# A two-layer transformer kernel on one core: the first batch's stack transfers, the weight pieces and the raw score pairs laid out anew over the steps of phase 1

## Reference

```python
# layer 0: gated MLP with quantised hidden values and ternary weight
scale = cond @ norm_w.T + 1.0
h = x * (scale[:, None, :] * rsqrt(mean(x * x) + EPS))
val, gate = split(h @ up_w.T, 2)
h = val * gelu(gate)
x = act_quant(h) @ weight_quant(down_w).T + x
# layer 1: attention over 16 heads of width 16, then a SwiGLU MLP
a = gamma * rmsnorm(x) + beta
q, k, v = a @ W_q.T, a @ W_k.T, a @ W_v.T
x = x + alpha * (softmax(scale * q @ k.T) @ v) @ W_o.T
f = gamma2 * rmsnorm(x) + beta2
x = x + alpha2 * ((silu(f @ gate_w.T) * (f @ hidden_w.T)) @ out_w.T + out_b)
```

## Time and profile before

| what | value |
|---|---|
| three timed runs | 1126.82, 1130.36, 1130.57 us; median 1130.36 us |
| profiled execution | 1129.7 us, its span from the first to the last instruction 1127.9 us |
| mean granted PE clock of the span | 0.961 |
| busy in the span | PE 1050.0 us (93%), DVE 770.8, ACT 578.9, POOL 293.8 |
| phase 1 | 0 to about 279.6 us |

### The profile page before, as it was taken

One profiled execution on the slowest core, in us unless ns is written; L12 is line 12 of the kernel. 1 busy time (PEld: TensorE's weight loads), 2 busy tenths in 40 slices (PEclk: granted clock), 3 DMA queues, 4 the chain that ended last, 5 costly groups with the idle time before them and its releaser, 6 DMA issues.

```text
span 1127.9 us, 18491 instructions
## 1 busy us (share of the span) xinstructions
PE 1050.0 (93%) x5864; PEld 659.5 (58%) x5864; DVE 770.8 (68%) x1224; ACT 578.9 (51%) x1168; POOL 293.8 (26%) x280
## 2 busy tenths in 40 slices
PE   6999999996899999989999998999999899899868
PEld 4777777764433545655664565566456556645656
DVE  5877776885565687668658767865876686676132
ACT  5577765553454456455445535654564464356221
POOL 2344442220000132232213223222322232032233
PEclk9999999997999999999999999999999999979889
DMA  9232217111430613224050323405032240500100
GB/s 286 86 94 75 76 57 131 62 52 39 76 48 11 109 18 41 72 55 56 10 117 15 42 69 58 56 10 117 17 40 71 56 56 10 99 1 2 52 0 19
DMA packets 58800, 66.65 MB, mean 59 GB/s; under 512 B 10992, under 2 KB 43832, under 8 KB 58752
## 3 DMA queue, kind: packets, MB, share of 16 engines
q1 hardware_dynamic: 44160, 48.80, 20.4%
q10 hardware_dynamic: 14592, 17.25, 7.9%
HBM read 27.73 MB, written 12.61 MB: 36 GB/s over the span
## 4 chain that ended last, share of the span: by engine, by line
PE 80%; DMA 9%; DVE 6%; issue 2%; ACT 2%; POOL 0%; ACTq 0%; SPq 0%; POOLq 0%; DVEq 0%
PE bank L1092 18%; PE bank L359 14%; PE bank L945 10%; PE bank L926 10%; PE bank L1136 9%; DMA k_stack<-hid 6%; PE raw_pair L885 6%; PE bank L810 4%; PE bank L861 2%; PE bank L382 2%; DVE rowmax L893 2%; PE bank L1208 2%; PE bank L403 1%; DMA k_stack<-split 1%; DMA up_st<-up_wT 1%
## 5 line engine op out<-in xcount | busy, mean ns | idle before, releaser
L934 ACT ACTIVATE probs<-bank 128x512 f32<-128x512 f32 x512 | 282.5, 598 | 250.6 <-PE bank L926 248.4
L893 DVE TENSOR_REDUCE rowmax<-raw_pair 128x2 f32<-128x1024 f32 x256 | 313.2, 1223 | 133.9 <-PE raw_pair L885 133.9
L885 PE MATMUL raw_pair<-k_stack,q_stack 48*128 48x512 f32 x512 | 178.2, 471 | 35.1 <-DMA k_stack<-hid 17.8
L359 PE MATMUL bank<-up_w,xs_part 128*128 128x512 f32 x768 | 199.9, 411 | 5.2 <-POOL xs_part L337 5.1
L926 PE MATMUL bank<-q_stack,k_stack 50*128 50x512 f32 x512 | 196.4, 455 | 1.4 <-issue 1.2
L359 PEld LDWEIGHTS bank<-up_w,xs_part 128*128 128x128 f32 x768 | 144.4, 194 | 38.3 <-POOL xs_part L337 5.9
L945 PE MATMUL bank<-probs,v_ext 128*17 128x512 f32 x1024 | 140.8, 622 | 0.3
L926 PEld LDWEIGHTS bank<-q_stack,k_stack 50*128 50x128 f32 x512 | 81.4, 190 | 81.5 <-issue 57.6
L1122 POOL TENSOR_TENSOR hid<-scratch,hid 128x512 fp32r<-128x512 f32 x64 | 82.4, 1288 | 159.3 <-ACT hid L1118 159.3
L1092 PE MATMUL bank<-xf_part,gate_w 128*128 128x512 f32 x384 | 109.1, 421 | 4.9 <-POOL xf_part L1082 4.1
L1092 PEld LDWEIGHTS bank<-xf_part,gate_w 128*128 128x128 f32 x384 | 69.2, 193 | 69.5 <-issue 52.8
(11 more groups left out here) (127 smaller groups left out, 1259.2 us busy)
## 6 DMA issues: line engine op xcount, KB each, us to landing
q_stack<-split SPq DMA_DIRECT2D x48, 128.0 KB, 4.7
q_stack<-hid SPq DMA_DIRECT2D x48, 128.0 KB, 5.3
xk<-xT SPq DMA_DIRECT2D x32, 128.0 KB, 2.0
xt<-x_tok SPq DMA_DIRECT2D x32, 128.0 KB, 2.5
x_spill<-x1t ACTq DMA_DIRECT2D x32, 128.0 KB, 1.7
xa_spill<-xa ACTq DMA_DIRECT2D x32, 128.0 KB, 2.2
x_in<-xa_spill SPq DMA_DIRECT2D x8, 512.0 KB, 5.2
k_stack<-split ACTq DMA_DIRECT2D x32, 128.0 KB, 7.9
```

The costliest lines, as they stand in the source:

```text
L359: last = nc.tensor.matmul(bank[j][:], xs_part[a][:, m % 2, k, :], up_w[w][:, k, col + j * W:col + (j + 1) * W], start=(i == 0), stop=(i == ...
L885: mm = nc.tensor.matmul(raw_pair[:, half, :], q_stack[rows, slot, qt * P:(qt + 1) * P], k_stack[rows, slot, :], start=True, stop=True)
L893: nc.vector.reduce_max(rowmax[:, e:e + RAWS + 1:RAWS], raw_pair[:], AX.X).then_inc(raw_read, 1)
L934: nc.scalar.activation(probs[:, (kt % 2) * J + j, :], score_bank[c % 3][:], ACT.Exp).then_inc(exp_done, 1)
```

## The change

The change touches phase 1 alone. The weight pieces keep one a step at steps 3 and 4 and go two a step from step 5 to step 11, and the last at step 12 (before: one a step, steps 3 to 19). The load, split, fill and projection of batch 0 are four steps earlier (the load one step). The stack transfers of SP are spread: two ahead of the loads in each of steps 19 to 22; ACT's four go two a step at steps 19 and 20. The raw pairs go one a step from step 23 to step 33 (before: steps 25 to 34, with two at step 32). In steps 0 and 1 the first slice of the up weight (`up_high_act(0)`, `up_low_dve(0)`) goes behind the first tile's scaling instead of ahead of it.

```diff
-        HIGH_AT = 3
-        LOW_AT = HIGH_AT + 1
-        XA_AT, SPLIT_AT, ONES_AT, QK_AT, STACK_AT = 12, 17, (21, 22), (20, 21), 23
-        RAW_STEPS = {25: 1, 26: 1, 27: 1, 28: 1, 29: 1, 30: 1, 31: 1, 32: 2, 33: 1, 34: 1}
+        def pieces_at(n):
+            return [i for i in range(len(PIECES)) if n == (3 + i if i < 2 else 5 + (i - 2) // 2)]
+        XA_AT, SPLIT_AT, ONES_AT, QK_AT, STACK_AT = 11, 13, (15, 16), (16, 17), 19
+        RAWS_AT = 23
         def raws_before(n):
-            first = sum(count for step, count in RAW_STEPS.items() if step < n)
-            return range(first, first + RAW_STEPS.get(n, 0))
+            return (n - RAWS_AT,) if 0 <= n - RAWS_AT < AHEAD else ()
+        STACK_SP = [(0, half, r) for half in range(2) for r in range(ROWS // HD)] + [(1, half, 0) for half in range(2)]
...
-            elif n == STACK_AT:
+            elif 0 <= n - STACK_AT < 4:
                 sp.wait_ge(stack_ones, 2)
-                stack_sp(sp, 0, (0, 0))
+                for w, half, r in STACK_SP[2 * (n - STACK_AT):2 * (n - STACK_AT) + 2]:
+                    sp.wait_ge(pair_free[w], credited(pair_free[w], 1))
+                    stack_dma(sp, 0, w, half, r)
...
             if n == 0:
                 load_small_act(act)
-                up_high_act(act, 0)
             elif n == 1:
-                for i in range(1, len(CHUNKS)):
+                for i in range(len(CHUNKS)):
                     up_high_act(act, i)
-            if 0 <= n - HIGH_AT < len(PIECES):
-                late_high_act(act, n - HIGH_AT)
+            for i in pieces_at(n):
+                late_high_act(act, i)
...
-            if 0 <= n - LOW_AT < len(PIECES):
-                late_low_pool(pool, n - LOW_AT)
+            for i in pieces_at(n - 1):
+                late_low_pool(pool, i)
```

More of the change, by code:

```diff
@@ L746, in before_dve @@
                 scale_dve(dve)
-                up_low_dve(dve, 0)
             elif n == 1:
-                for i in range(1, len(CHUNKS)):
+                for i in range(len(CHUNKS)):
                     up_low_dve(dve, i)
```

## The result

The changed kernel took 1118.42 us in the median (1114.58 to 1119.71, five runs), the kernel before, beside it on the same chip, 1129.96 us (1125.93 to 1130.57): a ratio of 0.9906, with a 95% interval from 0.9878 to 0.9934. It is faster by more than 0.5%. The forecast was 1121.0 us, range 1117 to 1126. A second measurement of the same kernel (last experiments) gave 1120.89 us against 1127.53 (0.9944 [0.9911, 0.9976]), that is between 0.2 and 0.9% less. Two slow executions of the kernel before (1132.37 and 1135.92 us) are left out of the second comparison.

A forecast was written before the change was run, and what follows sets the result against it. PE was taken to bound phase 1, with holes at steps 23 and 32. Gains of 2.49, 5.08 and 1.48 us sum to 9.05: profiled 1129.7 becomes 1120.65, 1121.3 as median; forecast 1121.0, range 1117.0 to 1126.0.

The forecast's parts named there:

- to the start of step 22 (pieces, head, first transfers): Start of phase 1: doubled weight pieces, reordered first weight slice and spread stack transfers, each priced at 0.
- step 22 to the pair of step 33: Ten steps of 7.78 us, then 7.35 us to the pair: 255.77 instead of 264.82, 9.05 us less.
- drain, from there to the first score: End of phase 1, 14.8 us with PE mostly waiting: change taken as 0, bounded by 1.5 us either way.
- Rival 1: Stack's stall stays in another step, contention with the loads being the cause: 3.6 us not regained, 1124.6; chance 0.09.
- rival 5: Change does less: a pair still waits as DVE runs late in step 30, 3 us, 1124.0; chance 0.03.
- second hole: Step 32: second raw pair waits 4.57 us for the first's maximum; 5.08 us plus 1.48 of slow clock to regain.
- first hole: Step 23: PE runs dry on a late tile load; 3.6 us of stall and slow clock regained, net 2.49.
- The load of tile 23 stands behind eight stack transfers: On SP: load goes out at 176.89, behind transfers beginning at 171.07; tile scaled 6.65 us after issue.
- are the same instructions in other steps: Preparations moved four steps earlier; POOL's heaviest becomes step 15, with a split and a fill, covered by idle time.
- Rival 3: Doubled weight pieces on POOL block DVE in each of seven steps: 8.3 us in all, 1129.3; chance 0.04.
- Rival 2: Gain given back to the clock in drain and phase 2: two more slow groups, 3.0 us, 1124.0; chance 0.10.
- rival 4: Spread transfers delay loads, PE stalls in each of steps 19 to 22, 3.6 us each: 1135.4; chance 0.03.

The follow-up runs named there:

- old_raws: Changed kernel with the raw pairs at the steps of before (25 to 34, two at step 32); 1128.69 us, ratio 1.0001.
- single_raws: Kernel before with one raw pair a step, steps 25 to 35, and nothing else; 1125.79 us, ratio 0.9968.
- block19: Changed kernel with SP's eight stack transfers as one block ahead of the loads of tile 19; 1119.85 us, ratio 0.9907.
- block21: Changed kernel with SP's eight stack transfers as one block ahead of the loads of tile 21; 1120.05 us, ratio 0.9911.
- late_fill_spread: Changed kernel with the fills of ones late (second at step 18), transfers still two a step; 1120.02 us, ratio 0.9923.
- late_fill_block: Changed kernel with the fills of ones late (second at step 18) and SP's eight transfers in one block at step 19; 1124.87 us, ratio 0.9979.
- late_fill_again: Same kernel as late_fill_block, no further edit, profiled a second time; profiled execution 1122.51 us.
- pieces_only: Kernel before with the weight pieces two a step and nothing else of the change; 1130.08 us, ratio 1.0037.

## Why the prediction was right

| term of the forecast | forecast | first profile after | second profile |
|---|---|---|---|
| to the start of step 22 (pieces, head, first transfers) | 0 | -1.45 us | +0.16 us |
| step 22 to the pair of step 33 | -9.05 us | -9.10 us | -9.07 us |
| drain, from there to the first score | 0, bound 1.5 | -0.42 us | -0.37 us |
| phase 2 | 0 | -4.13 us | -2.82 us |

**The sum of step 22 to step 33** held to 0.05 us in both profiles: one pair a step gives steps of 7.78 us, both holes are closed, the shift on DVE at step 30 costs nothing, and the slow clock goes with the holes. Rival 1 (the stall stays) and rival 5 (a pair still waits) did not come. For the second hole, two pairs in one step on one buffer, the reason was right too: `old_raws` brings it back (a wait of 4.56 us) and `single_raws` takes it out.

**The reason for the first hole was half the reason.** The step "The load of tile 23 stands behind eight stack transfers" named the order on SP, and rival 1 set contention against it as an alternative. The runs show that both were needed: with a late load that finds most transfers landed (`block19`), or transfers on their way and an early load (`block21`, `late_fill_spread`), there is no hole; with both (`late_fill_block`) there is. Nor was it the eight issues that made the load late, but SP's wait for k's low part inside the block. The change removes both at once, by the spread and by the earlier fill, so the forecast's number came out, in this part by luck; in the changed schedule, either the spread or the earlier fill could be left out at no cost. That the preparations moved earlier "are the same instructions in other steps" passed over what the fill holds back on SP, and passed over that the fill moved by six steps and not by four.

**The pieces** were priced at 0 and cost 0.2 us, once, by a mechanism that I had weighed and put at zero because in the one step with two POOL operations DVE idled. The idle time was ahead of DVE's gate product, which reads one operand from a bank of the matmuls; the operation that was held up is another, the rounding behind it, on which PE waits sooner. Rival 3's 8.3 us are far off.

**Clock.** Rival 2 (3 us given back) shows in neither profile, since phase 2 got no longer; but 3 us are less than what phase 2 varies by. The 4.13 us by which phase 2 is shorter in the first profile are not evidence of a gain: two profiles of one kernel (`late_fill_block` and `late_fill_again`) have a phase 2 of 841.73 and 849.83 us, 8.1 apart. The three profiles with the stack transfers of before (before, `single_raws`, `pieces_only`) have 848.3 to 849.9, the other eleven 841.7 to 849.8 with a median of 846.6, so a small real difference is possible and not settled. The medians differ by 11.5 us in the first measurement and 6.6 in the second, on either side of the forecast's 9.05. That the first median (1118.42) lies 2.6 us under the forecast is within this.

**One stall did not become four** (rival 4): two transfers take 1.2 to 1.6 us of SP in each of four steps, against 1.3 in the forecast, and steps 19 to 21 take 7.18 to 7.23 us.

## What to carry to other kernels

A hole on the engine that bounds the kernel can need two causes at once; putting the suspected one back alone, as `block19` did, tells whether it was the cause or only one of two. When a load is late, read both its time of issue and its time from issue to landing, and give each its own explanation: here the first came from a wait inside the block of transfers, and the second from transfers that were issued before the load and had not landed. A buffer used once a step and handed back once a step must not be asked for twice in one: here that cost more (5.1 us and 1.5 of slow clock) than the transfers did.

## What the runs showed of the hardware

- The same 128 KB load, issued at the same place of the program, landed after 4.0 us where two transfers of 128 KB of SP had still to land at its issue (`block19`), and after 6.2 us where five had (`late_fill_again`). In the kernel before, the six transfers of q were issued within 3.3 us and landed 3.5 us (the first) to 5.6 us (the sixth) after their issue: one every 1.1 us, though issued every 0.65.
- DVE's rounding of 128x1024 took 0.75 us alone and 1.20 us where a POOL operation on two tensors of 128x512 ran for the first 0.65 us of it. It shows as a longer instruction and not as idle time of DVE.
- The group of 12 matmuls in step 4, early in phase 1, was granted the full level in 3 of 14 profiles and the lower one for a part of it in the others (4.3 to 5.4 us instead of 3.05), with no edit that went with it.
- The length of phase 2 varied by 8.1 us between two executions of one kernel. In the first 100 us of it the granted clock was 0.97 in the short one and 0.88 in the long one. A single profile's span says little about a change below 1%; its steps do.
